# Rotary and chunked attention: the mask moves from TensorE products into VectorE's row minima, a batch is normalized one quad earlier, and chunk attention's rows are normalized by GpSimd

## The reference

```python
q = apply_rope(split_heads(x @ Wq)); k = apply_rope(split_heads(x @ Wk)); v = split_heads(x @ Wv)
sim = jnp.einsum('bid,bjd->bij', q, k) * scale
sim = jnp.where(causal[None], sim, -jnp.inf)
attn = jax.nn.softmax(sim, axis=-1)
out = jnp.einsum('bij,bjd->bid', attn, v)
return out.transpose(...) @ Wo + bo
```

## Time and profile before

| what | value |
|---|---|
| median of 3 runs | 4226.66 us (4223.68 to 4236.27) |
| the profiled execution | 4221.0 us, span 4219.3 us |
| busy share of the span | PE 85%, PEld 53%, DVE 63%, ACT 55%, POOL 47% |
| TensorE in 300 to 500 us (chunk attention) | 191.16 of 200 us |
| TensorE in 1500 to 2000 us (rotary attention) | 485.06 of 500 us |

### The profile page before, as it was taken

The page is one execution under the profiler, slowest core; times in us unless marked ns, Lnnn a source line. Parts: engine busy times, 40 slices in busy tenths (PEclk is TensorE's granted clock), DMA queues, the critical chain, the costliest instruction groups (busy, mean ns, idle before and its releaser), DMA issues. The chain is left out here.

```text
span 4219.3 us, 89135 instructions
## 1 busy us (share of the span) xinstructions
PE 3577.8 (85%) x31200; PEld 2222.9 (53%) x31295; DVE 2677.2 (63%) x5798; ACT 2302.2 (55%) x5504; POOL 1990.1 (47%) x1991
## 2 busy tenths in 40 slices
PE   5999999966858999999999999996857776787768
PEld 1333333325854556656565565555755665575546
DVE  6888888855445666666666666655455665555465
ACT  2766776753324556555555555553325553575367
POOL 2222222217435666666666666757431111565175
PEclk8999999985878999999999999995878997897879
DMA  5333333301551112111111111122542222110001
GB/s 98 58 58 58 58 58 58 58 28 59 184 160 45 47 41 50 42 44 48 42 47 44 41 47 45 44 54 60 182 145 63 68 65 50 33 62 6 1 1 41
DMA packets 418236, 252.24 MB, mean 60 GB/s; under 512 B 251186, under 2 KB 344354, under 8 KB 416642
## 3 DMA queue, kind: packets, MB, share of 16 engines
q1 hardware_dynamic: 409156, 228.56, 23.3%
q0 software_dynamic: 8640, 17.97, 1.3%
HBM read 75.12 MB, written 41.75 MB: 28 GB/s over the span
## 5 line engine op out<-in xcount | busy, mean ns | idle before, releaser
L2496 POOL TENSOR_TENSOR ra_prob<-ra_prob,ra_inverse 128x256 f32<-128x256 f32 (+3 forms) x512 | 630.6, 1253 | 472.0 <-DVE ra_inverse L2719 472.0
L2655 ACT ACTIVATE ra_prob<-ra_ps_s,ra_low 128x128 f32<-128x128 f32 (+3 forms) x1024 | 535.0, 530 | 320.6 <-DVE ra_low L2700 320.2
L2311 DVE TENSOR_REDUCE ca_mx<-ca_ps_s 128x2 f32<-128x1024 f32 x512 | 600.6, 1211 | 112.7 <-PE ca_ps_s L2172 112.4
L2237 ACT ACTIVATE ca_pT<-ca_ps_p 128x512 f32<-128x512 f32 x1024 | 548.8, 603 | 219.6 <-PE ca_ps_p L2182 195.0
L2700 DVE TENSOR_REDUCE ra_low<-ra_ps_s 128x2 f32<-128x256 f32 (+3 forms) x512 | 406.4, 815 | 77.5 <-PE ra_ps_s L2599 76.2
L2172 PE MATMUL ca_ps_s<-ca_kst,ca_qst 128*128 128x512 bf16 x991 | 381.2, 390 | 49.9 <-DVE ca_mx L2311 28.2
L2707 DVE TENSOR_TENSOR ra_prod<-ra_ps_r,ra_cos 128x512 f32<-128x512 f32 x256 | 176.6, 690 | 313.4 <-PE ra_ps_r L2561 265.2
L2182 PE MATMUL ca_ps_p<-ca_qst,ca_kst 128*128 128x512 bf16 x962 | 362.5, 382 | 4.9 <-ACT ca_pT L2237 4.5
L2536 PE MATMUL ra_ps_t<-ident,ra_prob 128*128 128x128 f32 x2560 | 352.9, 276 | 3.0 <-ACT ra_probT L2661 1.8
L2661 ACT COPY ra_probT<-ra_ps_t 128x512 f32<-128x512 f32 x384 | 226.4, 590 | 235.0 <-PE ra_ps_t L2536 234.9
L2489 POOL TENSOR_TENSOR ra_rot<-ra_prod 128x512 f32<-128x512 f32 x256 | 320.9, 1275 | 62.9 <-DVE ra_prod L2708 62.7
(11 more groups left out here) (413 smaller groups left out, 7162.2 us busy)
## 6 DMA issues: line engine op xcount, KB each, us to landing
moe_w_own<-moe_w1T SPq DMA_DIRECT2D x142, 256.0 KB
ra_qz<-ra_rot SPq DMA_DIRECT2D x512, 64.0 KB, 2.0
ra_kz<-ra_rot SPq DMA_DIRECT2D x512, 64.0 KB, 2.0
ca_kst<-ca_bounce SPq DMA_DIRECT2D x256, 64.0 KB
ca_bounce<-ca_thirds SPq DMA_DIRECT2D x192, 64.0 KB, 2.9
ca_qst<-ca_bounce SPq DMA_DIRECT2D x64, 192.0 KB
moe_hs<-moe_rows SPq DMA_DIRECT2D x142, 66.0 KB
moe_raw<-in_L_ffn_W SPq DMA_DIRECT2D x32, 256.0 KB, 3.2
```

The source lines that it names most:

```text
L2237: nc.scalar.activation(pT[:, (NS * hp + u) % PRING, :], ps_p[n % NP][:], ACT.Exp).then_inc(sg["drained"], 1)
L2311: nc.vector.tensor_reduce(mx[:, hm % 2, 2 * j:2 * j + 2], ps_s[m % 2][:].rearrange("p (b k) -> p b k", b=2), AX.X, ALU.max)\
L2496: nc.gpsimd.tensor_tensor(at, at, inverse[:, n % PROB, 2 * tile:2 * tile + 2].unsqueeze(2).broadcast_to([P, 2, keys]), ALU.mult)\
L2655: nc.scalar.activation(prob[:, n % PROB, tile, head, 0:keys], part(n, tile)[:, head, :], ACT.Exp, bias=low[:, n % PROB, at:at + 1], scale= ...
```

## The change

- `mask` becomes a float32 tile of 128x512 whose last 128 columns hold the mask. `masks` is gone; `scores` writes alone. `minima` uses `tensor_tensor_reduce` for each head and tile: it adds the mask's last (tile + 1) * 128 columns to the scores, writes the sum back to `ra_ps_s` and takes its minimum. There are eight per pair in place of four reductions, and each compiles into two instructions, the operation and one that writes out the minimum.
- `exponentials(tile, n)` becomes `exponential(tile, head, n)`: in slot 0 head 0 of tiles 0 and 1, in slot 1 head 1 of both.
- `coming` is the quad before `batch`. Statistics, power and normalized rows move there (rows in slot 7 now); the bias stays in `batch`, at slot 3 for slot 7.
- Chunk attention's `norm.apply` goes from VectorE (pair 12) to GpSimd, behind the two powers.
- VectorE, no longer TensorE, waits for the prepared mask at the stage's start.

```diff
@@ chunk_attention, gpsimd
                         for c in range(2):
                             norm.rstd(pool, 2 * h + c, c)
+                        for c in range(2):
+                            t = 2 * h + c
+                            pool.wait_ge(norm.rstd_done, t + 1)
+                            nc.gpsimd.tensor_scalar(tile_of(xn, t), tile_of(X, t), norm.mv[:, c, 0:1], norm.rs[:, c:c + 1], ALU.subtract, ALU.mult)\
+                                .then_inc(sg["x_normed"], 1)
@@ chunk_attention, vector
                         for c in range(2):
+                            wait(dve, sg["x_normed"], 2 * h + c - 1)
                             norm.stats(dve, 2 * h + c, c, tile_of(X, 2 * h + c))
-                    if j == 12:
-                        for c in range(2):
-                            dve.wait_ge(norm.rstd_done, 2 * h + c + 1)
-                            norm.apply(tile_of(xn, 2 * h + c), tile_of(X, 2 * h + c), c).then_inc(sg["x_normed"], 1)
@@ rope_attention
-        mask = sb("mask", [P, P], BF16)
+        mask = sb("mask", [P, S])
-            for k in range(-1, QUADS + OUT):
+            for k in range(-2, QUADS + OUT):
-                    batch = (k + 1) // NQ if (k + 1) % NQ == 0 and k + 1 < QUADS else None
+                    batch = (k + 1) // NQ if (k + 1) % NQ == 0 and 0 <= k + 1 < QUADS else None
+                    coming = (k + 2) // NQ if (k + 2) % NQ == 0 and k + 2 < QUADS else None
@@ gpsimd
-                    if batch is not None and j == 3:
-                        pool.wait_ge(sg["var_done"], batch + 1)
-                        nc.gpsimd.tensor_tensor(rs[:], var[:], core.minus_half[:, 0:TC], ALU.pow).then_inc(sg["rs_done"], 1)
-                    if batch is not None and j == 5:
-                        pool.wait_ge(sg["rs_done"], batch + 1)
-                        wait(pool, sg["x_turned"], batch)
-                        for c in range(TC):
-                            nc.gpsimd.tensor_scalar(xn[:, c, :], X[:, batch * TC + c, :], mv[:, c, 0:1], rs[:, c:c + 1], ALU.subtract, ALU.mult)\
-                                .then_inc(sg["x_normed"], 1)
-                    if batch is not None and j == 7:
+                    if coming is not None and j == 3:
+                        pool.wait_ge(sg["var_done"], coming + 1)
+                        nc.gpsimd.tensor_tensor(rs[:], var[:], core.minus_half[:, 0:TC], ALU.pow).then_inc(sg["rs_done"], 1)
+                    if coming is not None and j == 7:
+                        pool.wait_ge(sg["rs_done"], coming + 1)
+                        wait(pool, sg["x_turned"], coming)
+                        for c in range(TC):
+                            nc.gpsimd.tensor_scalar(xn[:, c, :], X[:, coming * TC + c, :], mv[:, c, 0:1], rs[:, c:c + 1], ALU.subtract, ALU.mult)\
+                                .then_inc(sg["x_normed"], 1)
+                    if batch is not None and j == 3:
                         pool.wait_ge(sg["x_normed"], TC * (batch + 1))
@@ tensor
-                            nc.tensor.matmul(diagonals, core.identb[:], mask[:].unsqueeze(1).broadcast_to([P, 2, P]), start=True, stop=False, skip_group_check=True)
-                            nc.tensor.matmul(part(n, t)[:, head, t * P:], core.identb[:], mask[:], start=True, stop=False, skip_group_check=True)
-                                                    start=False, stop=True, skip_group_check=True)
+                                                    start=True, stop=True)
@@ scalar
-                        exponentials(0, score)
+                        for tile in (0, 1):
+                            exponential(tile, 0, score)
@@ vector
-                    for tile in (0, 1) if t == 0 else (t,):
-                        nc.vector.tensor_reduce(low[:, n % PROB, 2 * tile:2 * tile + 2], part(n, tile), AX.X, ALU.min).then_inc(sg["low_done"], 1)
+                    for head in range(2):
+                        for tile in (0, 1) if t == 0 else (t,):
+                            at, scored = 2 * tile + head, part(n, tile)[:, head, :]
+                            nc.vector.tensor_tensor_reduce(scored, scored, mask[:, S - (tile + 1) * P:], 1.0, BIGGEST, ALU.add, ALU.min, low[:, n % PROB, at:at + 1])\
+                                .then_inc(sg["low_done"], 1)
-                    if batch is not None and j < TC:
+                    if coming is not None and j < TC:
```

More of the change, by code:

```diff
@@ L2381, in rope_attention @@
     TC = S // P
-    MASKED = 1e30
+    MASKED, BIGGEST = 1e30, 3e38
     SLOTS = 2 * TC
@@ L2441, in slots @@
                     out = k - OUT if 0 <= k - OUT < QUADS else None
-                    batch = (k + 1) // NQ if (k + 1) % NQ == 0 and k + 1 < QUADS else None
-                    body(j, t, s, front, score, value, out, batch)
+                    batch = (k + 1) // NQ if (k + 1) % NQ == 0 and 0 <= k + 1 < QUADS else None
+                    coming = (k + 2) // NQ if (k + 2) % NQ == 0 and k + 2 < QUADS else None
+                    body(j, t, s, front, score, value, out, batch, coming)
         with nc.Block() as block:
@@ L2462, in move, with body @@
                             sp.dma_start(to[at:at + HALF, n % RING, :], rot[h * HALF:(h + 1) * HALF, front % 2, o, x, :]).then_inc(qk_ready[n % RING], 16)
-                def body(j, t, s, front, score, value, out, batch):
+                def body(j, t, s, front, score, value, out, batch, coming):
                     if front is None or j not in (3, 5):
@@ L2478, in _ @@
                 pool.wait_ge(prep, 1)
-                nc.gpsimd.affine_select(out=mask[:], in_=mask[:], compare_op=ALU.is_ge, fill=MASKED, base=0,
+                nc.gpsimd.affine_select(out=mask[:, S - P:], in_=mask[:, S - P:], compare_op=ALU.is_ge, fill=MASKED, base=0,
                                         pattern=[[-1, P]], channel_multiplier=1).then_inc(prep, 1)
@@ L2581, in turn_rows, with scores @@
                     last.then_inc(sg["x_turned"], 1)
-                def masks(t, n):
+                def scores(t, n):
                     if t == 0:
@@ L2629, in body @@
                     if score is not None and t == 2:
-                        for tile in (2, 3):
-                            masks(tile, score)
                         for tile in (2, 3):
@@ L2646, in _, with exponential @@
                             .then_inc(w_ready, 1)
[L2648 to L2656, removed]
+                def exponential(tile, head, n):
+                    keys, at = (tile + 1) * P, 2 * tile + head
+                    act.wait_ge(sg["low_done"], SLOTS * n + (2 * (head + 1) if tile < 2 else at + 1))
+                    if (tile, head) == (0, 0):
+                        wait(act, sg["p_turned"], FILLS * (n - PROB + 1))
+                        wait(act, sg["inverse_done"], 2 * (n - PROB + 1))
+                    nc.scalar.activation(prob[:, n % PROB, tile, head, 0:keys], part(n, tile)[:, head, :], ACT.Exp,
+                                         bias=low[:, n % PROB, at:at + 1], scale=-1.0, accum_out=total[:, n % PROB, at:at + 1]).then_inc(sg["exp_done"], 1)
                 def fill(i, n):
@@ L2679, in body @@
                     if score is not None and t == 1:
-                        exponentials(1, score)
+                        for tile in (0, 1):
+                            exponential(tile, 1, score)
                     if value is not None and t == 2:
@@ L2687, in body @@
                     if score is not None and t == 3:
-                        exponentials(2, score)
-                        exponentials(3, score)
+                        for tile in (2, 3):
+                            for head in range(2):
+                                exponential(tile, head, score)
                 slots(body)
@@ L2694, in _ @@
                 dve.wait_ge(loaded, 80)
+                dve.wait_ge(prep, 2)
                 def minima(t, n):
```

16 lines of the change are left out of this document (4 added, 12 removed).

## The result

| | before | changed |
|---|---|---|
| median of 4 runs | 4229.05 us (4223.68 to 4236.27) | 4108.51 us (4105.47 to 4111.71) |
| span of the profiled execution | 4219.3 us | 4108.3 us |

The ratio is 0.9714, 95% interval 0.9696 to 0.9732: 121 us faster, where 42 were forecast and the range ended at 4130. On another chip the changed kernel came to 0.9728 (0.9715 to 0.9741).

The account below looks back on a forecast made before the run. The prediction took TensorE's work in a row to bound the kernel, with one sizeable wait of 43.1 us. Its terms, 43 + 1 - 11 + 10 - 1 = 42 us, gave 4179, stated as 4180, range 4130 to 4222.

Parts of the forecast that it names:

- The minima: Rotary attention: mask products leave TensorE, but dearer minima delay fill(1) in slots 0 and 1; 0.02 us a quad, 1 us gained.
- slack of 0.40: Slots 0 and 1: fill(1) ended at 2054.48, turn(3) on TensorE needed it at 2054.88, so 0.40 us to spare.
- The wait: Rotary attention: TensorE's 15 waits of 2.9 us for GpSimd's normalized rows go entirely, 43 us gained.
- The statistics: Rotary attention: ra_var's 1.05 us instruction, a quad earlier, makes fill(1) later; 0.75 us, 15 times, 11 us lost.
- Chunk attention: Normalized rows moved from VectorE to GpSimd save 0.3 us in each of 32 halves, 10 us (0 to 22).
- The 1 us at its start: Chunk attention's first half: GpSimd's rows are on the path where nothing else runs; about 1 us lost.
- Half rate: Rival: VectorE's new minima take two cycles per element; kernel 110 us slower, about 4330; chance 0.10.
- The accumulation costs as on ScalarE: Rival: minimum's write-out costs r = 0.20 us; no change, or 4211 with chunk attention's 10 us; chance 0.17.
- The write-out is cheap: Rival: r = 0.09 us or less and chunk attention gives its full 22; sum 84 us, 4137; chance 0.28.
- the prediction's formula: A quad gains 0.62 - 2d us, where d is how late turn(3) on TensorE starts; times 64 quads.
- the 41 us: Gain of the parts other than the minima, set against the loss from a late turn(3).
- a quad of 22.2 us or below, the copy was not late: Sign: a quad at 22.2 us or below means fill(1) was not late and the write-out was priced too high.

Follow-up runs that it names:

- experiment 5: The changed kernel with fill(1) on VectorE put between the minima of head 0 and head 1 in slots 0 and 4: 0.968 of the kernel before.
- experiment 6: The changed kernel with four short 128x1 memsets on VectorE ahead of each fill(1): 0.9741 of the kernel before.
- experiment 10: The changed kernel with one product of two 128x512 tiles on VectorE ahead of each fill(1): 0.9967 of the kernel before, median 4204.74 us.
- experiment 4: The kernel before with two unused float32 products of 128x512 put into TensorE's wait for the normalized rows: 0.9943.
- experiment 1: The kernel before with only the batch's statistics, power and normalized rows moved a quad earlier: 0.9868, median 4161.11 us.
- experiment 11: The kernel before with the normalizing moved a quad earlier and ra_var made by a reduction reading one SBUF tensor: 0.9836.
- experiment 3: The kernel before with only the mask moved from TensorE's products into VectorE's minima: 0.9909, median 4180.37 us.

## Why the prediction was wrong

Faster was right, and the wait for the rows went as named. But the sum was 42 us and the measured drop 115 to 121: the mask's part, which the prediction put at 1 us, was 36, and two more terms were mis-sized to the same side.

- **The minima (term 1 us, measured 36).** The step that failed is the price r of a minimum's write-out, 0.14 us forecast and 0.04 measured, and in it the lower bound "at least a short VectorE instruction's step, 0.09 us": the write-out starts together with the next operation. So VectorE is 0.30 us later at fill(1), not 0.70.
- **Two smaller errors in the same term, partly against each other.** With 0.30 us the prediction's slack of 0.40 would have let slots 0 and 1 gain 0.10 a pair, and the quad 0.8 us or 52 in all; the two slots lost 0.03 a pair. The slack was 0.27 to 0.29 us, because turn(3) starts 0.05 us behind the copy's end and its four products take 0.06 longer than half of eight. And the 0.31 us of a mask product's place was worth 0.21 (experiment 5); that slots 2 and 3 gained the forecast 0.3 all the same is luck, since the projection behind the wait ran 0.1 shorter. The slope is right: 0.09 us late costs 0.18 a quad (experiment 6), 0.61 and 0.69 cost 1.28 (experiment 10).
- **The wait (term 43 us, measured 61).** "The whole wait goes: 43 us" was right, and the transposes behind it no longer wait for anything. What was left out is what follows the wait: TensorE's clock falls behind 8 of the 15 waits, 18 us (experiment 4). It was in the trace to be had: I read one quad that ends a batch and took it for all.
- **The statistics (term -11 us, measured +9).** I took the 1.05 us of `ra_var` for the instruction's price. It is a wait for a division on GpSimd. With the normalizing moved alone it costs 0.6 us in each of 15 quads (experiments 1 and 11), 9 us. In the kernel before it costs the same in the quads that end a batch. From projection 4 to the output projection it is 5.43 us in the quad of the earlier trace rows and 4.81 (2061.86 to 2066.67) in that of the earlier trace rows:

```profile
2012.14 1.12 PE L2561 MATMUL ra_ps_r<-ra_xT,ra_w 128*128 128x512 f32 x2
...
2017.57 2.02 PE L2571 MATMUL ra_ps_r<-ra_wo,ra_oT 128*128 128x128 f32 x16
...
2066.67 2.02 PE L2571 MATMUL ra_ps_r<-ra_wo,ra_oT 128*128 128x128 f32 x16
```

In the changed kernel VectorE comes to `ra_var` a little later against GpSimd's division, its median is 0.22 us, and the 9 us are saved. With the mask moved alone it is 0.22 too. These 9 us, less some 5 of the clock's that experiments 1 and 3 both save, are what hangs together in their sum.

- **Chunk attention (10 us forecast, 9 to 12 measured)** was right. The 1 us at its start can't be told: its first transpose on VectorE is at 100.5 us for 101.4, and at 99.6 to 103.4 over all kernels here.
- **The rivals.** Half rate fell on the first row of the trace. "The accumulation costs as on ScalarE" is what experiment 10 imitates. There a quad is 0.72 us longer than before the change, and the prediction's formula gives about as much for a copy that late; the kernel is still at 0.9967, because the other parts are worth about twice the 41 us that it set against it. "The write-out is cheap" came nearest; its 4137 lacked the clock's 18 us, 16 of the statistics and 9 of the mask, and had 10 too many in chunk attention.
- **What would have shown it.** The prediction named "a quad of 22.2 us or below, the copy was not late". The quad is 22.23, and the copy is late all the same: the length alone did not settle it, experiment 5 did.

Add up by the traces: 64 x 0.56 = 36 for the mask; 15 x 4.8 = 72 for what a quad that ends a batch had beyond a plain one and its 0.6 us of transposes (43 the wait, 18 the clock, 9 the statistics, 1 the transposes themselves); 2 in the first quads: 110, rotary attention's whole difference.

## What to carry to other kernels

When a stall recurs, list all its instances before pricing one: quads with the same 2.9 us wait were 4.1, 5.8 and 7.1 us longer than the others. Where one engine has no time to spare, a copy that another engine makes for it too late comes back one for one once the slack is used; splitting the work so that the copy goes in between gave 24 us for a few moved lines. A tiny instruction with a long duration may be waiting, not working; look at what ends with it.

## What the runs showed of the hardware

- A minimum folded into a two-tensor operation, with its source read from PSUM and written back there, costs 311 ns at 128 columns and 707 at 512, against 292 and 692 for a plain sum. Its write-out's 142 ns overlap the next operation entirely; the four in slot 0 take 1.22 us with theirs.
- TensorE's granted clock fell to 0.50 behind some of the 2.88 us waits and not behind others of the same length (8 of 15), and behind none once 1.9 us of products stood in them. Which of the waits it follows was not settled; in the kernel before they came in a fixed order, two of four, and with the mask moved alone, where the waits are 3.4 us, in every second one.
- A 128x4 VectorE instruction, as a tensor_scalar or with two SBUF sources, took 1.04 to 1.05 us and ended with GpSimd's instruction in progress; a tensor_reduce with the same result took 0.16, with GpSimd as busy. A 128x512 one with two SBUF sources took up to 1.6 us for 0.69.
